# A gated adapter kernel in split fp32: W_up loaded by slot behind the first rows, its halves made by ACT and GpSimd, a new order for the first tiles and the tail

## The chip, the core and the metric

The kernel runs on one NeuronCore of a Trainium2 chip. Its engines are TensorE (PE, matrix products into PSUM), VectorE (DVE), ScalarE (ACT), GpSimd (POOL) and SyncE (SP, which here only issues DMAs). Each engine takes its instructions in the order in which they are written and waits on semaphores of the others. The metric is the device time of one execution in microseconds.

## What is computed

For each of 64 sequences (64 rows of 512 values) an expert index from 0 to 2 picks one set of adapter weights. All is fp32:

```python
Wd = W_down[stream]; bd = b_down[stream]; Wu = W_up[stream]
bu = b_up[stream]; g = ln_w[stream]; b = ln_b[stream]
residual = hidden_states
h = jnp.einsum('bsh,bhk->bsk', hidden_states, Wd) + bd[:, None, :]
h = jax.nn.gelu(h, approximate=False)
h = jnp.einsum('bsk,bkh->bsh', h, Wu) + bu[:, None, :]
h = residual + h
mean = jnp.mean(h, axis=-1, keepdims=True)
var = jnp.mean(jnp.square(h - mean), axis=-1, keepdims=True)
h = (h - mean) * jax.lax.rsqrt(var + LN_EPS)
return h * g[:, None, :] + b[:, None, :]
```

W_down is 512x256 and W_up 256x512 for each of the three experts.

## The kernel before, in words

**Tiles.** Two sequences of the same expert make a tile of 128 rows. The kernel sorts the sequences by expert on the chip (DVE and one small product, over at about 7 us), which gives 33 tiles in 66 slots. `io_table` holds the sequence of each slot, `tile_expert` the expert of each tile. Since tiles are sorted, W_up is kept by slots: slot 0 holds the expert of the first tile, `wu_from` says which experts the slots take.

**Precision.** Every factor is split into a high part (rounded to fp32r) and a low part (the rest), and a product is made of three: high x high, high x low, low x high. So W_down and W_up need a `wd_hi`/`wd_lo` and `wu_hi`/`wu_lo` of 128x1024 each per expert. Before the loop, all of this must be made from what the DMAs bring.

**One tile t** passes through these steps. PE `transpose_x(t)` (4 instructions) writes xT; ACT `x_hi` copies the high half and DVE `x_lo` makes the low one; PE `down(t)` makes 12 products into `h`; DVE `down_bias` adds the bias to `hb`; ACT `gelu` makes g; PE `transpose_g` (2); ACT `g_hi`, DVE `g_lo`; POOL `add_bias` makes xb = x + b_up; ACT `seed` copies xb into the PSUM bank of y; PE `up(t)` adds 6 products to it; DVE `stats`, `mean_var`, `variance`; POOL `power` makes rstd; DVE `scale` makes (y - mean) * ln_w into `scaled`; ACT `rescale` multiplies by rstd into `normed` (2 buffers); POOL `shift` adds ln_b into `res`; SP and ACT store one half each. The last two tiles take a shorter end on DVE, `shift_last`.

**Order.** Each engine's order is written by hand. PE does in body(t): transpose_g(t), down(t+1), transpose_x(t+3), up(t). ACT does in body(t): seed(t), g_hi(t-1), a store, gelu(t), x_hi(t+2), rescale(t-3), where rescale(k) waits for scaled(k), rstd(k) and, since normed has two buffers, for shift(k-2). POOL does in body(t): shift(t-1), power(t), add_bias(t+4). DVE does in body(t): stats(t-1), g_lo(t), down_bias(t+1), mean_var(t-1), variance(t-1), x_lo(t+2), scale(t-1). In front of these loops stand the first tiles by hand, between the copies of the weights.

**The weights in front.** ACT issues the loads of W_down and the first half of expert 0 of W_up; SP issues, behind the first x rows, the rest of W_up by expert (L244), then x rows, ln_w (L311), ln_b. ACT makes wd_hi of expert 0, POOL (L251) that of 1 and 2. ACT waits until all of W_up has landed, then makes the three wu_hi (L469); DVE makes all wd_lo (L256) and wu_lo (L686) and the down bias rows (L614). POOL's add_bias for tile 1 waits for the first wu_lo.

## Time and profile before

| | us |
|---|---|
| median of 3 executions | 142.57 |
| the three | 140.57, 142.57, 143.46 |
| the profiled execution | 140.62 |
| its span, first to last instruction | 138.5 |
| PE busy in it | 126.7 (91%) |
| DVE busy | 114.8 (83%) |
| POOL busy | 106.3 (77%) |
| ACT busy | 83.2 (60%) |

What lies around the span is 2.1 us. Two stages are to be told apart: up to about 30 us, weights and first rows arrive and PE works with gaps; from then on, PE runs one tile behind another without a gap up to 130 us; then a tail of 8 us. A busy share is a mean over all three, so the waits have to be read stage by stage. Of the DMA, 21.9 MB moved, at 293 to 350 GB/s from 3.5 to 24 us and at about half of that or less later.

### The profile page before, as it was taken

To read this page: it belongs to the slowest core of one execution; us is meant where nothing else is said; L and a number is where in the kernel's file an instruction comes from. 1 tells how busy PE (TensorE), PEld (TensorE's weight loads), DVE (VectorE), ACT (ScalarE), POOL (GpSimd) and SP (SyncE) were. 2 spreads that over 40 slices of the span, in tenths; PEclk is the share of its full clock that TensorE was granted. 3 is DMA by queue.
4 is the path that set the end of the run, shared out by engine and by line. 5 is a ranking of instruction groups with operands and counts; after the bars stand their busy time and mean duration, and the time that the engine had idled before them with its cause. 6 is when DMAs were issued, how large, how long until landed. Compare 5 with 4: busy or idle time off the path is not lost.

```text
span 138.5 us, 4090 instructions
## 1 busy us (share of the span) xinstructions
PE 126.7 (91%) x848; PEld 112.3 (81%) x849; DVE 114.8 (83%) x278; ACT 83.2 (60%) x174; POOL 106.3 (77%) x113
## 2 busy tenths in 40 slices
PE   6886888989999999999999999999999999999820
PEld 6785757859999999999999999999999999998610
DVE  1899595998888799888988897889788978897982
ACT  0834558457766666666666666766666666666600
POOL 7096049509888888888888889888888898889770
PEclk9999999999999999999999999999999999999995
DMA  1989999544233545555544555445546633332465
GB/s 39 331 293 325 350 300 301 159 122 146 80 116 114 156 145 157 146 158 145 151 160 126 163 161 163 153 151 151 151 151 151 151 76 76 80 76 51 98 167 143
DMA packets 13216, 21.94 MB, mean 158 GB/s; under 512 B 2313, under 2 KB 3858, under 8 KB 13202
## 3 DMA queue, kind: packets, MB, share of 16 engines
q1 hardware_dynamic: 8674, 15.48, 37.7%
q10 hardware_dynamic: 4528, 6.31, 16.4%
q8 instruction: 4, 0.07, 0.2%
q14 instruction: 10, 0.08, 0.2%
HBM read 13.39 MB, written 8.65 MB: 159 GB/s over the span
## 4 chain that ended last, share of the span: by engine, by line
PE 69%; DVE 7%; DMA 6%; ACT 4%; issue 3%; POOL 3%; DVEq 2%; SPq 2%; POOLq 1%; ACTq 0%
PE hg_ps L814 29%; PE y_ps L847 27%; PE xT_ps L800 9%; PE hg_ps L823 5%; DMA wu<-in_L_cond_W_up_dram 5%; POOL res L384 2%; DMA itok_all_i<-in_itok_B_dram 2%; DVE wu_lo L686 2%; ACT wu_hi L469 1%; DVE hb L637 1%; DVEq L607 1%; DVE r_stats L649 1%; SPq L241 1%; DVEq L61 1%; SPq L244 1%
## 5 line engine op out<-in xcount | busy, mean ns | idle before, releaser
L384 POOL TENSOR_TENSOR res<-normed,lnb_rows 128x512 f32<-128x512 f32 x31 | 40.0, 1290 | 15.3 <-ACT normed L465 15.1
L367 POOL TENSOR_TENSOR xb<-x_sb,bu_rows 128x512 f32<-128x512 f32 x33 | 44.7, 1356 | 6.6 <-DVE wu_lo L686 5.5
L445 ACT ACTIVATE g<-hb 128x256 f32<-128x256 f32 x33 | 13.8, 418 | 37.7 <-DVE hb L637 37.7
L649 DVE BATCH_NORM_STATS2 r_stats<-y_ps 128x6 f32<-128x512 f32 x33 | 23.0, 695 | 6.0 <-issue 5.1
L670 DVE SCALAR_TENSOR_TENSOR scaled<-y_ps,r_mv,lnw_rows 128x512 f32<-128x512 f32 x33 | 24.5, 743 | 0.1
L847 PE MATMUL y_ps<-wu_hi,gT_hi 128*128 x66 | 23.4, 435 | 0.7 <-ACT gT_hi L450 0.7
L814 PE MATMUL hg_ps<-wd_hi,xT_hi 128*128 x132 | 23.9, 303 | 0.0
L629 DVE TENSOR_TENSOR xT_lo<-xT_ps,xT_hi 128x512 fp32r<-128x512 f32 x33 | 22.8, 689 | 0.3 <-ACT xT_hi L440 0.2
L465 ACT ACTIVATE normed<-scaled,rstd 128x512 f32<-128x512 f32 x31 | 22.4, 724 | 0.0
L800 PE MATMUL xT_ps<-ident,x_sb 128*128 128x128 f32 x132 | 20.0, 274 | 1.8 <-DMA x_sb<-in_x_dram 1.8
L847 PE MATMUL y_ps<-wu_lo,gT_hi 128*128 x66 | 20.8, 397 | 0.4 <-DVE wu_lo L686 0.4
L814 PE MATMUL hg_ps<-wd_hi,xT_lo 128*128 x132 | 21.0, 281 | 0.0
L847 PE MATMUL y_ps<-wu_hi,gT_lo 128*128 x66 | 20.8, 396 | 0.2 <-DVE gT_lo L643 0.2
L814 PE MATMUL hg_ps<-wd_lo,xT_hi 128*128 x132 | 20.9, 281 | 0.0
L457 ACT COPY y_ps<-xb 128x512 f32<-128x512 f32 x33 | 19.5, 590 | 1.6 <-POOL xb L367 1.5
L440 ACT CAST xT_hi<-xT_ps 128x512 fp32r<-128x512 f32 x33 | 18.8, 571 | 2.0 <-PE xT_ps L800 2.0
L373 POOL TENSOR_TENSOR rstd<-var_eps,half_neg 128x1 f32<-128x1 f32 x33 | 18.1, 550 | 1.6 <-DVE var_eps L658 1.6
L637 DVE TENSOR_TENSOR hb<-hg_ps,bd_rows 128x256 f32<-128x256 f32 x33 | 14.0, 423 | 5.3 <-PE hg_ps L814 4.8
L814 PEld LDWEIGHTS hg_ps<-wd_hi,xT_hi 128*128 128x128 f32 x132 | 17.8, 189 | 0.1
L814 PEld LDWEIGHTS hg_ps<-wd_hi,xT_lo 128*128 128x128 f32 x132 | 17.9, 188 | 0.0
L814 PEld LDWEIGHTS hg_ps<-wd_lo,xT_hi 128*128 128x128 f32 x132 | 17.8, 188 | 0.0
L800 PEld LDWEIGHTS xT_ps<-ident,x_sb 128*128 128x128 f32 x132 | 15.0, 140 | 2.9 <-DMA x_sb<-in_x_dram 1.9
(85 smaller groups left out, 146.0 us busy)
## 6 DMA issues: line engine op xcount, KB each, us to landing
x_sb<-in_x_dram SPq DMA_DIRECT2D x64, 128.0 KB, 2.7
out_dram<-res ACTq DMA_DIRECT2D x33, 128.0 KB, 2.4
out_dram<-res SPq DMA_DIRECT2D x33, 128.0 KB, 2.3
wd<-in_L_cond_W_down_dram ACTq DMA_DIRECT2D x3, 512.0 KB, 4.8
wu<-in_L_cond_W_up_dram SPq DMA_DIRECT2D x2, 512.0 KB, 5.6
...
```

The lines of the kernel that those rows point to most:

```text
L367: pool.tensor_tensor(xb[:, c % DEEP, :], x_sb[:, c % FAR, :], bu_rows[:, ds(e * H, H)], ALU.add).then_inc(xb_ready, 1)
L373: pool.tensor_tensor(rstd[:, c % DEEP:c % DEEP + 1], var_eps[:, c % DEEP:c % DEEP + 1], half_neg[:], ALU.pow).then_inc(rstd_ready, 1)
L384: pool.tensor_tensor(res[:, c % FAR, :], normed[:, c % PAR, :], lnb_rows[:, ds(e * H, H)], ALU.add).then_inc(res_ready, 1)
L440: act.copy(xT_hi[:, c % PAR, :], xT_ps[c % PAR][:]).then_inc(xhi_ready, 1)
L457: act.copy(y_ps[c % YBANKS][:], xb[:, c % DEEP, :]).then_inc(seeded, 1)
L465: act.activation(normed[:, c % PAR, :], scaled[:, c % DEEP, :], ACT.Copy, scale=rstd[:, c % DEEP:c % DEEP + 1]).then_inc(normed_ready, 1)
L629: dve.tensor_tensor(xT_lo[:, c % PAR, :], xT_ps[c % PAR][:], xT_hi[:, c % PAR, :].bitcast(F32), ALU.subtract).then_inc(xlo_ready, 1)
L649: dve.bn_stats(r_stats[:, c % DEEP, :], y_ps[c % YBANKS][:]).then_inc(stats_ready, 1)
L670: dve.scalar_tensor_tensor(out=scaled[:, c % DEEP, :], in0=y_ps[c % YBANKS][:], scalar=r_mv[:, c % DEEP, 0:1], in1=lnw_rows[:, ds(e * H, H ...
L800: mm = pe.transpose(xT_ps[c % PAR][:, k * P:(k + 1) * P], x_sb[:, c % FAR, k * P:(k + 1) * P], ident[:])
L814: mm = pe.matmul(h, x_half[:, c % PAR, k * P:(k + 1) * P], w_half[:, ds(w0 + k * BN, BN)], start=(w_half is wd_hi and x_half is xT_hi and ...
L847: mm = pe.matmul(y_ps[c % YBANKS][:], g_half[:, c % PAR, k * P:(k + 1) * P], w_half[:, ds(w0 + k * H, H)], start=False, stop=(n == 2 and k ...
```

## The change

W_up is no longer loaded by expert ahead of all but the first rows. SP waits until the sort is done, reads `wu_from`, and loads slot by slot, with x rows in between and a semaphore for each slot: slot 0, x of tile 2, slot 1, x of tiles 3 and 4, slot 2, x of tile 5, ln_w, x of tile 6, ln_b. ACT makes all `wd_hi`, the down bias rows, two of the three up bias rows, and all `wu_hi` as each slot lands; DVE makes the third up bias row, all `wd_lo` and `wu_lo` of slot 0; POOL makes `wu_lo` of slots 1 and 2, behind add_bias(2) and add_bias(3). The first tiles have a new written order on PE, ACT and DVE; scale(0) (the first user of ln_w) and rescale(0) to rescale(2) stand later. In the sort one link of the chain goes. In the tail, the last two tiles are scaled in place in PSUM, `shift_last` of the second-last tile moves ahead of stats of the last, rescale moves ahead of the last gelu and power ahead of a shift.

The diff, cut to its core:

```diff
 SP
-            load_w_up(sp, 0, 1, KB)
-            for e in range(1, E):
-                load_w_up(sp, e, 0, KB)
+            sp.wait_ge(slots_ready, 2)
+            sp.reg_load(from_regs, wu_from[0:1, 0:E])
+            from_expert = [sp.snap(reg, min_val=0, max_val=E - 1 - slot) + slot for slot, reg in enumerate(from_regs)]
+            load_w_up(sp, 0, from_expert[0])
             load(2, 2, entries(2, 0, 2))
-            sp.dma_start(lnw_rows[:], rows_of(ln_w, P)).then_inc(lnw_in, 16)
+            load_w_up(sp, 1, from_expert[1])
             for t in range(3, 5):
                 load(t, t, entries(t, 0, 2))
+            load_w_up(sp, 2, from_expert[2])
+            load(5, 5, entries(5, 0, 2))
+            sp.dma_start(lnw_rows[:], rows_of(ln_w, P)).then_inc(lnw_in, 16)
+            load(6, 6, entries(6, 0, 2))
             sp.dma_start(lnb_rows[:], rows_of(ln_b, P)).then_inc(lnb_in, 16)
...
 POOL
-            for e in range(1, E):
-                w_down_high(pool, e).then_inc(wd_hi_rest, 1)
-            pool.wait_ge(bu_ready, E)
-            add_bias(0, 0)
-            pool.wait_ge(wu_lo_ready, 1)
-            for t in range(1, DEEP):
+            pool.wait_ge(bu_last_ready, 1)
+            pool.wait_ge(bu_ready, E - 1)
+            for t in range(3):
                 add_bias(t, t)
+            w_up_low(pool, 1).then_inc(wu_lo_rest, 1)
+            add_bias(3, 3)
+            w_up_low(pool, 2).then_inc(wu_lo_rest, 1)
...
 ACT
+            wd_high(1)
             for t in range(2):
                 load_half(act, t, 1, act.snap(head_regs[3 * t], min_val=0, max_val=B - 1))
-            for e in range(E):
-                keep_up_bias(e)
+            wd_high(2)
+            for part in range(len(bd_banks)):
+                keep_down_bias(part)
             x_hi(0, 0)
+            keep_up_bias(0)
             x_hi(1, 1)
-            seed(0, 0)
+            keep_up_bias(1)
+            wu_high(0)
             gelu(0, 0)
-            act.wait_ge(wu_in, 16 * (E + 1))
-            wu_high(0, sources[0])
+            seed(0, 0)
             g_hi(0, 0)
             x_hi(2, 2)
-            wu_high(1, sources[1])
+            wu_high(1)
+            gelu(1, 1)
+            g_hi(1, 1)
+            x_hi(3, 3)
+            seed(1, 1)
+            gelu(2, 2)
+            x_hi(4, 4)
+            seed(2, 2)
+            wu_high(2)
...
+            seed(4, 4)
+            rescale(0, 0)
+            g_hi(4, 4)
+            gelu(5, 5)
+            x_hi(7, 7)
+            seed(5, 5)
+            rescale(1, 1)
+            rescale(2, 2)
...
 DVE (front)
             x_lo(0, 0)
-            dve.wait_ge(bd_ready, len(bd_banks))
+            dve.wait_ge(up_spread, E)
+            dve.tensor_copy(bu_rows[:, (E - 1) * H:E * H], y_ps[E - 1][:]).then_inc(bu_last_ready, 1)
             x_lo(1, 1)
+            dve.wait_ge(bd_ready, len(bd_banks))
             down_bias(0, 0)
...
-            wu_low(0, sources[0])
+            w_up_low(dve, 0).then_inc(wu_lo_first, 1)
             g_lo(0, 0)
             down_bias(1, 1)
             x_lo(2, 2)
-            wu_low(1, sources[1])
...
 DVE (tail)
             stats(last - 1, last - 1)
-            g_lo(last, last)
             dve.wait_ge(stats_ready, last)
             mean_var(last - 1, last - 1)
             variance(last - 1, last - 1)
-            scale(last - 1, last - 1, e_last[1])
+            g_lo(last, last)
+            scale_last(last - 1, e_last[1])
+            shift_last(last - 1, e_last[1])
             stats(last, last)
             dve.wait_ge(stats_ready, last + 1)
             mean_var(last, last)
             variance(last, last)
-            scale(last, last, e_last[0])
-            shift_last(last - 1, e_last[1])
+            scale_last(last, e_last[0])
             shift_last(last, e_last[0])
...
 PE
-            body(1, 1)
+            e_up, e_down = experts_from(1)
+            down(2, 2, e_down)
+            transpose_g(1, 1)
+            transpose_x(4, 4)
+            up(1, 1, e_up)
             body(2, 2)
```

**Order on ACT, tiles 3 to 6.** ACT before, from g_hi(2) to g_hi(4). In the names, gT_hi is g_hi, g is gelu, xT_hi is x_hi, y_ps is seed (its number is the tile modulo 4) and normed is rescale:

```order
L450 CAST gT_hi<-hg_ps0 128x256 [waits gT_ready]
L445 ACTIVATE g<-hb 128x256 [waits hb_ready]
L440 CAST xT_hi<-xT_ps1 128x512 [waits xT_ready]
L465 ACTIVATE normed<-scaled,rstd 128x512 [waits rstd_ready,scaled_ready]
L457 COPY y_ps0<-xb 128x512 [waits scaled_ready,xb_ready]
L450 CAST gT_hi<-hg_ps1 128x256 [waits gT_ready]
L445 ACTIVATE g<-hb 128x256 [waits hb_ready]
L440 CAST xT_hi<-xT_ps0 128x512 [waits xT_ready]
L465 ACTIVATE normed<-scaled,rstd 128x512 [waits rstd_ready,scaled_ready]
L457 COPY y_ps1<-xb 128x512 [waits scaled_ready,xb_ready]
L450 CAST gT_hi<-hg_ps0 128x256 [waits gT_ready]
```

and in the changed kernel, from gelu(4) to g_hi(5):

```order
L444 ACTIVATE g<-hb 128x256 [waits hb_ready]
L439 CAST xT_hi<-xT_ps0 128x512 [waits xT_ready]
L456 COPY y_ps0<-xb 128x512 [waits scaled_ready,xb_ready]
L464 ACTIVATE normed<-scaled,rstd 128x512 [waits rstd_ready,scaled_ready]
L449 CAST gT_hi<-hg_ps0 128x256 [waits gT_ready]
L444 ACTIVATE g<-hb 128x256 [waits hb_ready]
L439 CAST xT_hi<-xT_ps1 128x512 [waits xT_ready]
L456 COPY y_ps1<-xb 128x512 [waits scaled_ready,xb_ready]
L464 ACTIVATE normed<-scaled,rstd 128x512 [waits rstd_ready,scaled_ready]
L464 ACTIVATE normed<-scaled,rstd 128x512 [waits res_ready,rstd_ready,scaled_ready]
L456 COPY y_ps2<-xb 128x512 [waits scaled_ready,xb_ready,slots_ready]
L449 CAST gT_hi<-hg_ps1 128x256 [waits gT_ready]
```

Before, one rescale stands in each tile (rescale(0) behind gelu(3), rescale(1) behind gelu(4)); now rescale(0) stands behind seed(4), and rescale(1) and rescale(2) stand together behind seed(5), both ahead of seed(6) and g_hi(5).

**Order on POOL, tiles 0 to 2 of its loop.** POOL in the changed kernel (it is the same as before here, but for line numbers; res is shift, rstd is power, xb is add_bias):

```order
L381 TENSOR_TENSOR res<-normed,lnb_rows 128x512
L370 TENSOR_TENSOR rstd<-var_eps,half_neg 128x1 [waits var_ready]
L208 TENSOR_LOAD tile_expert
L364 ISA [waits seeded,x_in5]
L364 TENSOR_TENSOR xb<-x_sb,bu_rows 128x512
L208 TENSOR_LOAD tile_expert
L381 ISA [waits normed_ready]
L381 TENSOR_TENSOR res<-normed,lnb_rows 128x512
L370 TENSOR_TENSOR rstd<-var_eps,half_neg 128x1 [waits var_ready]
L208 TENSOR_LOAD tile_expert
L364 ISA [waits seeded,x_in6]
L364 TENSOR_TENSOR xb<-x_sb,bu_rows 128x512
```

Behind shift(0) stand power(1) and add_bias(5), behind shift(1) power(2) and, next, add_bias(6).

**Order on POOL in front.** Before, from the copies of W_down to add_bias(1):

```order
L251 CAST wd_hi<-wd 128x1024 [waits wd_in1]
L251 CAST wd_hi<-wd 128x1024 [waits wd_in2]
L207 TENSOR_LOAD tile_expert [waits bu_ready,slots_ready]
L367 ISA [waits x_in0]
L367 TENSOR_TENSOR xb<-x_sb,bu_rows 128x512
L207 TENSOR_LOAD tile_expert [waits wu_lo_ready]
L367 ISA [waits x_in1]
L367 TENSOR_TENSOR xb<-x_sb,bu_rows 128x512
```

and now, from add_bias(2) to power(0):

```order
L208 TENSOR_LOAD tile_expert
L364 ISA [waits x_in2]
L364 TENSOR_TENSOR xb<-x_sb,bu_rows 128x512
L258 TENSOR_TENSOR wu_lo<-wu,wu_hi 128x1024 [waits wu_hi_ready]
L208 TENSOR_LOAD tile_expert
L364 ISA [waits x_in3]
L364 TENSOR_TENSOR xb<-x_sb,bu_rows 128x512
L258 TENSOR_TENSOR wu_lo<-wu,wu_hi 128x1024 [waits wu_hi_ready]
L370 TENSOR_TENSOR rstd<-var_eps,half_neg 128x1 [waits var_ready]
```

The two casts of W_down and the wait for DVE's first wu_lo are gone from POOL, and two subtractions of 128x1024 stand ahead of power(0).

## Rows read from the trace of the kernel before

**Rows 1.** Windows: us, busy and instructions of PE, PEld, DVE, ACT, POOL, clock, DMA.
```profile
40.00:130.00 90.00, 90.00 (x621) 81.61 (x619) 78.05 (x183) 59.93 (x130) 79.33 (x79) 1.00 0.47 131
...
134.00:135.00 1.00, 0.00 (x0) 0.00 (x0) 1.00 (x2) 0.00 (x0) 0.33 (x1) 0.83 0.67 205
```

**Rows 2.** Chain that ended last, around tile 4 (start us, us, what).
```profile
29.85 0.44 PE hg_ps L823 x2
...
33.64 0.22 PE hg_ps L823 x2
33.86 1.42 PE hg_ps L814 x12
35.27 0.44 PE xT_ps L800 x4
35.71 1.40 PE y_ps L847 x6
```

**Rows 3.** Timeline of ACT, tiles 3 to 6 (start us, us, instruction).
```profile
29.21 0.42 ACT L445 ACTIVATE g<-hb 128x256 f32<-128x256 f32 x1 [2.83 <-DVE hb L637]
...
30.00 0.72 ACT L465 ACTIVATE normed<-scaled,rstd 128x512 f32<-128x512 f32 x1
...
32.47 0.42 ACT L445 ACTIVATE g<-hb 128x256 f32<-128x256 f32 x1 [0.95 <-DVE hb L637]
...
34.06 0.59 ACT L457 COPY y_ps<-xb 128x512 f32<-128x512 f32 x1
...
37.36 0.59 ACT L457 COPY y_ps<-xb 128x512 f32<-128x512 f32 x1
...
37.87 0.37 ACT L450 CAST gT_hi<-hg_ps 128x256 fp32r<-128x256 f32 x1
```

**Rows 4.** Timeline of POOL, tiles 0 to 5.
```profile
30.96 1.29 POOL L384 TENSOR_TENSOR res<-normed,lnb_rows 128x512 f32<-128x512 f32 x1 [4.13 <-ACT normed L465]
32.20 0.55 POOL L373 TENSOR_TENSOR rstd<-var_eps,half_neg 128x1 f32<-128x1 f32 x1
32.73 1.30 POOL L367 TENSOR_TENSOR xb<-x_sb,bu_rows 128x512 f32<-128x512 f32 x1
34.16 1.29 POOL L384 TENSOR_TENSOR res<-normed,lnb_rows 128x512 f32<-128x512 f32 x1
```

**Rows 5.** Timeline of TensorE, tiles 0, 1 and 5.
```profile
12.22 0.66 PE L800 MATMUL xT_ps<-ident,x_sb 128*128 128x128 f32 x4 [0.20 <-DMA x_sb<-in_x_dram]
...
13.08 0.72 PE L814 MATMUL hg_ps<-wd_hi,xT_hi 128*128 x4
...
16.23 0.38 PE L823 MATMUL hg_ps<-ident,g 128*128 128x128 f32 x2
...
38.93 0.71 PE L847 MATMUL y_ps<-wu_hi,gT_hi 128*128 x2
```

**Rows 6.** POOL instructions of line L367: duration ns min/median/max.
```profile
L367 POOL TENSOR_TENSOR xb<-x_sb,bu_rows x33: 1278/1297/2274, 11.5 to 126.2; 128x512 f32<-128x512 f32 x33
```

**Rows 7.** Groups by line: xcount, busy us, mean ns, idle before.
```profile
L469 ACT CAST wu_hi<-wu 128x1024 fp32r (+1 forms) x3 | 3.1, 1049 | 0.5 <-DMA wu<-in_L_cond_W_up_dram 0.5
```

**Rows 8.** SP queue, start us and us of its issues.
```profile
7.29 1.29 SPq L241 DMA_DIRECT2D x_sb<-in_x_dram  x2
8.64 1.69 SPq L244 DMA_DIRECT2D wu<-in_L_cond_W_up_dram  x3
11.06 1.14 SPq L241 DMA_DIRECT2D x_sb<-in_x_dram  x2
```

**Rows 9.** DMA issues: KB each, median us from issue to landing.
```profile
x_sb<-in_x_dram SPq DMA_DIRECT2D x64, 128.0 KB, 2.7
...
wu<-in_L_cond_W_up_dram SPq DMA_DIRECT2D x2, 512.0 KB, 5.6
...
x_sb<-in_x_dram ACTq DMA_DIRECT2D x2, 128.0 KB, 3.5
```

**Rows 10.** Timeline of DVE, its last two instructions.
```profile
134.41 1.41 DVE L679 SCALAR_TENSOR_TENSOR res<-scaled,rstd,lnb_rows 128x512 f32<-128x512 f32 x2
```

More of the change, by code:

```diff
@@ L155, in adapter_program @@
         wd_in = [sem(f"wd_in{e}") for e in range(E)]
-        wu_in = sem("wu_in")
+        wu_in = [sem(f"wu_in{slot}") for slot in range(E)]
         biases_in = sem("biases_in")
@@ L301, in _ @@
             head_regs = [sp.alloc_register(f"head{i}") for i in range(4)]
+            from_regs = [sp.alloc_register(f"from{i}") for i in range(E)]
             sp.wait_ge(slots_ready, 1)
```

155 lines of the change are left out of this document (87 added, 68 removed).

## Prediction

> **What bounds the kernel now.** I read the busy times by stretch first: from 40 to 130 us PE is busy 90.00 of 90.00 us at full clock [rows 1]. The chain that ended last confirms it: transpose_g 0.22, down 1.42, transpose_x 0.44 (the step from there to 35.71), up 1.40, together 3.48 us per tile, with nothing between [rows 2]. No edit touches those instructions, so the kernel's time is when this run begins, plus what breaks it, plus the tail.
>
> It begins at transpose_g(3), 29.85 [rows 2]. PE's first product is at 13.08 [rows 5]. Up to 29.85 it has four downs, three ups, three transposes of g and four of x to do: 5.7 + 4.2 + 0.7 + 1.8 = 12.4 us in 16.8. So 4.4 us of waits can be won there at most, beside an earlier first product.
>
> Then I looked for what runs beside PE with little slack, since a hand-written order can break there. The timelines of ACT and POOL show a ring: rescale(0) at 30.00 [rows 3], shift(0) at 30.96, power(1) 32.20, add_bias(5) 32.73 to 34.03, shift(1) 34.16 [rows 4], seed(5) at 34.06, 0.03 behind add_bias(5), and seed(6) at 37.36, then g_hi(5) at 37.87 [rows 3], and up(5) at 38.93 [rows 5]. g_hi(5) is over at 38.24, so the ring stands 0.7 us ahead of PE. It is hidden, but nearly as long as PE's tile.
>
> **The change, front.** What it removes: POOL's two casts of W_down and its wait for DVE's wu_lo, two wu_lo and the down bias copies on DVE, and ACT's wait for all of W_up. What it adds to ACT: two more casts of 1.05 us [rows 7] and the bias copies. I walk it by tile.
>
> x of tile 1 has less ahead of it in the DMA queues (no part of W_up). The two x loads of ACT took 3.5 us to land, the median of all x loads is 2.7 [rows 9]: 0.8 us earlier, so transpose_x(1) is at 11.4 in place of 12.22, down(0) behind it by the same 0.86 at 12.3, and down(1) is over at 15.4 (3.15 us from 13.08 to 16.23 [rows 5]). The bounds are no gain (12.22) and, if a load takes 2.3, 11.0. ACT's third cast and the bias copies end before 11.4, behind W_down's last landing; that cover is about 0.3 us.
>
> Slot 0 of W_up: SP's x issues end at 8.58; a register load on SP takes about 0.7 (10.33 to 11.06), so it is issued at 9.3 [rows 8]. 512 KB take 5.6 under load [rows 9] and more likely somewhat less here, since the queues are emptier: landed at 14.0 (bounds 13.3 and 14.9). ACT: wu_high(0) 14.05 to 15.0, gelu(0) at once behind, 15.4. POOL's add_bias(0) waits for the last bias row from DVE (about 13.5) and a register load, 14.0 to 15.3; DVE's wu_lo(0) has two operands in SBUF and waits for it. I take that from add_bias itself, whose longest is 2.27 against a median of 1.30 [rows 6]: one of the two engines stood still there. wu_lo(0) is then done at 16.5. Seed(0) and g_hi(0) end at 16.4, up(0) runs 16.45 to 17.85.
>
> Then transpose_x(3) to 18.3, down(2) to 19.7, transpose_g(1) to 20.1. ACT does g_hi(1), x_hi(3), seed(1) in this order, about 0.4 + 0.5 + 0.6 (0.51 from a 512-column start to the next [rows 3]): PE waits 1.2 us, up(1) 21.6 to 23.0. ACT goes on with gelu(2), x_hi(4), seed(2) and wu_high(2), 22.8 to 23.9. Slot 2 has landed by then: SP issues it at about 16.0. POOL's subtraction for slot 2 starts at 23.9. The trace shows no 128x1024 subtraction on POOL; twice a 128x512 of 1.28 to 1.30 [rows 6] is 2.55 (bounds 2.1 and 3.0). It ends at 26.45, up(2)'s second pair of products waits for it, and transpose_g(3) follows 0.95 later: **27.4 in place of 29.85, a lead of 2.45 us**. With the bounds above the lead is 1.3 to 3.0.
>
> The Trainium skill (GPSIMD Engine Reference, "Elementwise — side-by-side cycle accounting") gives 4497 ns for such an add of 2048 columns; an estimate from it for 1024 is 2.25 us, and the lead by it would be 2.75. No row here shows that size.
>
> Behind this I cost at nothing: ln_w later (issued about 18.4; scale(0) stands at about 26.2, so the cover is near 1 us if it takes 7 us to land), ln_b (shift(0) is at 32), the shorter sort (one link of 0.2 us, some 0.1 of it won, behind the DMAs), DVE's later scale(0) to scale(2) (0.74 each, PE waits for none of them directly).
>
> **The change, the ring.** Here the new order costs. rescale(0) now stands behind gelu(4), x_hi(6) and seed(4), not behind gelu(3). Before, gelu(4) started 2.62 us after transpose_g(3) (32.47 against 29.85), and PE still paces it. From a gelu to the rescale behind it were 0.79 (29.21 to 30.00 [rows 3]); with a seed between, 0.79 + 0.51 = 1.30. So rescale(0) is at transpose_g(3) + 3.92. From there the old trace gives each step: to shift(0) 0.96, to power(1) 1.24, to add_bias(5) 0.53, its own 1.30 and 0.03 to seed(5), 4.06 in all [rows 3, 4]; seed(5) to rescale(1) 0.51; the same 4.06 again over shift(1), power(2), add_bias(6) to seed(6); 0.51 to g_hi(5), 0.37 for it and 0.1 to PE. Sum: 3.92 + 4.06 + 0.51 + 4.06 + 0.51 + 0.47 = 13.53. rescale(2) lies between, waits for power(2) and is over before add_bias(6) is. Before, up(5) started 38.93 - 29.85 = 9.08 behind transpose_g(3). **PE, which has nothing else to do ahead of up(5), stands still for 4.45 us once.** up(5) starts at 27.4 + 13.53 = 40.93, 2.0 us later than before. The lead is eaten and 2.0 more; with the bounds of the lead +1.45 to +3.15. Behind up(5) all goes on at 3.48.
>
> **The change, the clock.** Such a gap has a second price. PE's last product releases DVE at 132.6 [rows 10], and the granted clock of 134 to 135 us is 0.83 [rows 1]: full to 134.66, then the 1.2 GHz level, 2.1 us behind the last product. A gap of 4.45 us is twice that, so I expect the clock to have fallen when up(5) comes. How soon it comes back no row shows. The only stretch at half rate is the last 3.84 us; as long a stretch would cost 1.9 us, and nothing is the other bound. I take 1.5, nearer the upper one. The Trainium skill (TensorE: Matmul & The Clock Gate, "HAM oscillation") says that waits between bursts drop TensorE to half rate, and that it pays for this when work returns; the fall at 134.66 agrees.
>
> **The tail.** shift_last(31), one of two of 0.7 us [rows 10], moves ahead of stats(32); but it needs about 0.6 of the time between stats(31) and y(32), which g_lo(32) and scale_last(31) already fill, so stats(32) comes 0.6 later and the chain behind it is 0.7 shorter. Won: 0.1 (bounds 0 and 0.4).
>
> **Sum.** -2.45 + 4.45 + 1.5 - 0.1 = +3.4 us on the profiled execution's 140.62: **144.0**. That execution is at the low end of the three; the median is 1.95 higher, and the same sum against it gives 145.9. Nothing in the trace tells me which of the two a new median resembles, so I name the middle, **145.0**. As a ratio it is 2.4% slower.
>
> **Rivals.** (A) The gap comes but the clock holds: 144.0 - 1.5 = 142.5 on the profiled basis, 1.4% slower, within 2%. For it: the clock was full through all the smaller waits of the front. Against it: the fall at 134.66. 0.2. (B) On the other side, faster: the ring stays hidden and the lead is kept. 140.62 - 2.45 - 0.1 = 138.1, faster by 1.8%; with the lead's upper bound 137.5, 2.2%. It needs rescale(0) 4.45 us earlier against PE, before gelu(4); or power(2) would have to come without shift(1). It decides where transpose_g(3) is at or before 25.4: from there the stall is paid by the lead. Every bound of the walk together gives 26.8. 0.1. (C) The front doesn't win: if slot 0 lands at 14.9 and POOL's two subtractions take 3.0 each, transpose_g(3) is at 28.6, and the same ring gives 145.2 on the profiled basis, 3.2% slower. For it: W_up is issued later than before. 0.1. My forecast, gap and clock both: 0.6.
>
> **Chances.** Changes below about 2% can't be told from none here. The forecast's own range on the profiled basis is 141.5 to 145.7 (+1.45 to +3.15, clock 0 to 1.9, tail); its middle is at 2.4%, so of its 0.6 I put 0.42 beyond 2% and 0.18 within. A gives 0.2 within (0.01 beyond, rounded off), B 0.03 faster and 0.07 within, C 0.1 slower. Faster 0.03, raised to 0.05 for what I did not see; within 0.43; slower 0.52. The range of the time: 141.5 below, and 145.7 with the median's offset, 147.5, above.
>
> **What would show it.** Right: transpose_g(3) near 27.4; one gap of PE of 4 to 5 us ahead of up(5), with ACT waiting for POOL in rescale(2) and seed(6); granted clock under 1.00 in the slices behind it; PE without a gap after that. Wrong: up(5) within 3.5 us of up(4), or transpose_g(3) later than 28.6, or a wait of DVE for ln_w. If add_bias and shift overlap or rescale(0) comes before gelu(4) is through, the sum falls with the 4.45.

## The result and the profile after

The kernel after takes 145.5 us (median of 4 executions, 144.43 to 146.48), the kernel before beside it 141.72 (4 executions, 140.57 to 143.46): a ratio of 1.032, 95% interval 1.027 to 1.037. It is **slower by 3.2%**. The profiled execution of after took 146.48, its span is 144.3 us, 5.8 more than before's 138.5.

The page's slices of the kernel after (40 equal ones of 3.6 us, tenths of busy time; PEclk is the granted clock):

```profile
PE   6899896899619999999999999999999999999840
PEclk9999999999975899999999999999999999999999
```

One hole in PE, in slices 11 and 12; the clock is low from the end of the hole on, in slices 12 to 14. The windows (columns as in [rows 1]):

```profile
40.00:50.00 10.00, 7.35 (x30) 6.44 (x31) 4.77 (x13) 4.95 (x11) 7.61 (x8) 0.66 0.30 91
50.00:130.00 80.00, 80.00 (x555) 72.72 (x554) 69.17 (x162) 53.60 (x116) 70.11 (x69) 1.00 0.48 136
```

From 50 us on PE is again busy all the time, as before from 40 [rows 1]. The timeline rows around the hole, ACT first, then POOL, then PE (start us, us, what, idle before and who ended it); [rows 3 to 5] are their counterparts:

```profile
33.09 0.72 ACT L464 ACTIVATE normed<-scaled,rstd 128x512 f32<-128x512 f32 x1
37.13 0.59 ACT L456 COPY y_ps<-xb 128x512 f32<-128x512 f32 x1 [0.82 <-POOL xb L364]
37.66 0.72 ACT L464 ACTIVATE normed<-scaled,rstd 128x512 f32<-128x512 f32 x1
40.74 0.72 ACT L464 ACTIVATE normed<-scaled,rstd 128x512 f32<-128x512 f32 x1 [2.36 <-issue]
41.62 0.59 ACT L456 COPY y_ps<-xb 128x512 f32<-128x512 f32 x1 [0.17 <-POOL xb L364]
```

```profile
34.05 1.28 POOL L381 TENSOR_TENSOR res<-normed,lnb_rows 128x512 f32<-128x512 f32 x1 [4.28 <-ACT normed L464]
...
38.55 1.26 POOL L381 TENSOR_TENSOR res<-normed,lnb_rows 128x512 f32<-128x512 f32 x1 [1.45 <-ACT normed L464]
40.28 1.26 POOL L364 TENSOR_TENSOR xb<-x_sb,bu_rows 128x512 f32<-128x512 f32 x1
```

```profile
29.25 0.43 PE L870 MATMUL hg_ps<-ident,g 128*128 128x128 f32 x2
37.95 0.60 PE L847 MATMUL xT_ps<-ident,x_sb 128*128 128x128 f32 x4
42.65 1.22 PE L894 MATMUL y_ps<-wu_hi,gT_hi 128*128 x2 [4.10 <-ACT gT_hi L449]
48.26 0.60 PE L847 MATMUL xT_ps<-ident,x_sb 128*128 128x128 f32 x4
```

The ring of the prediction stands here link by link: rescale(0) 33.09, shift(0) 34.05, add_bias(5) 35.81, seed(5) 37.13, rescale(1) 37.66, shift(1) 38.55, add_bias(6) 40.28, seed(6) 41.62, g_hi(5) 42.15, up(5) 42.65. Between transpose_x(8), over at 38.55, and up(5) PE has nothing, 4.10 us. The chain that ended last runs through the same place:

```profile
39.77 0.55 POOL rstd L370
40.32 1.24 POOL xb L364
...
42.65 2.92 PE y_ps L894 x6
...
46.00 2.42 PE hg_ps L861 x12
```

Six products of an up take 2.92 us there and twelve of a down 2.42, where [rows 2] has 1.40 and 1.42: half rate for the up, and a little better for the down, since the full clock came back before its end. By microsecond (same columns as the windows above):

```profile
41.00:42.00 1.00, 0.00 (x0) 0.00 (x0) 0.00 (x0) 0.83 (x2) 0.91 (x2) 0.64 0.03 8
47.00:48.00 1.00, 1.00 (x7) 1.00 (x6) 0.00 (x0) 0.00 (x0) 1.00 (x1) 0.50 0.54 176
48.00:49.00 1.00, 1.00 (x9) 0.96 (x9) 0.43 (x2) 0.00 (x0) 0.07 (x1) 0.95 0.22 70
```

0.50 is the 1.2 GHz level. The clock fell at about 41.3, while PE stood still, and was back at 48.1 (both worked out from the shares 0.64 and 0.95).

**The 5.8 us add up.** transpose_g(3) is 0.60 earlier (29.25; 29.85 [rows 2]). up(5) starts 13.40 behind it in place of 9.08: + 4.32. From up(5) to transpose_x(9) it takes 5.61 (42.65 to 48.26); before, 3.12 (38.93 [rows 5] to the next row below): + 2.49. From there to the end of DVE's last res nothing changes. What is left, 0.4, lies behind DVE's last instruction, which ends 2.27 us ahead of the span's end now and 2.68 before ([rows 10]: 134.41 + 1.41). -0.60 + 4.32 + 2.49 - 0.41 = 5.80. Two rows of the kernel before that belong to this, transpose_x(9) and the stats of the last tile, which PE's last product released (0.27 us of waiting, so at 132.6; the prediction used it and pointed at [rows 10], where it doesn't stand):

```profile
42.05 0.60 PE L800 MATMUL xT_ps<-ident,x_sb 128*128 128x128 f32 x4
132.60 0.70 DVE L649 BATCH_NORM_STATS2 r_stats<-y_ps 128x6 f32<-128x512 f32 x1 [0.27 <-PE y_ps L847]
```

### The profile page after: what moved, and what is told of

Its sections match the earlier page's. It is cut to its first block, busy times and chain, and to the rows that moved or that the text cites. A ratio compares the mean times of both kernels' runs of the same rounds, so it can differ in the third digit from the quotient of the medians.

```text
span 144.3 us, 4085 instructions
## 1 busy us (share of the span) xinstructions
PE 130.2 (90%) x850; PEld 116.8 (81%) x851; DVE 111.7 (77%) x275; ACT 85.7 (59%) x177; POOL 106.4 (74%) x113
## 4 chain that ended last, share of the span: by engine, by line
PE 62%; POOL 4%; DVE 3%; issue 1%; ACT 1%; POOLq 1%; ACTq 1%; DVEq 0%
PE hg_ps L861 25%; PE y_ps L894 25%; PE xT_ps L847 7%; PE hg_ps L870 4%; POOL res L381 2%; DVE res L718 1%; POOL rstd L370 1%; POOL xb L364 1%; DVE y_ps L709 1%; POOLq L208 1%; ACT normed L464 0%; DVE r_stats L682 0%; ACTq L433 0%; DVE hb L670 0%; ACT y_ps L456 0%
## 5 line engine op out<-in xcount | busy, mean ns | idle before, releaser
L364 POOL TENSOR_TENSOR xb<-x_sb,bu_rows 128x512 f32<-128x512 f32 x33 | 43.7, 1326 | 12.6 <-ACT bu_rows L486 12.6
L894 PE MATMUL y_ps<-wu_hi,gT_hi 128*128 x66 | 23.9, 444 | 6.3 <-ACT gT_hi L449 5.1
L703 DVE SCALAR_TENSOR_TENSOR scaled<-y_ps,r_mv,lnw_rows 128x512 f32<-128x512 f32 x31 | 22.9, 743 | 0.0
L861 PE MATMUL hg_ps<-wd_lo,xT_hi 128*128 x132 | 21.4, 285 | 0.0
L676 DVE TENSOR_TENSOR gT_lo<-hg_ps,gT_hi 128x256 fp32r<-128x256 f32 x33 | 13.8, 418 | 7.8 <-ACT gT_hi L449 7.5
L861 PEld LDWEIGHTS hg_ps<-wd_hi,xT_hi 128*128 128x128 f32 x132 | 18.3, 194 | 0.3 <-issue 0.2
L861 PEld LDWEIGHTS hg_ps<-wd_lo,xT_hi 128*128 128x128 f32 x132 | 18.3, 192 | 0.0
```

What stands on the lines that cost most here:

```text
L364: pool.tensor_tensor(xb[:, c % DEEP, :], x_sb[:, c % FAR, :], bu_rows[:, ds(e * H, H)], ALU.add).then_inc(xb_ready, 1)
L703: dve.scalar_tensor_tensor(out=scaled[:, c % DEEP, :], in0=y_ps[c % YBANKS][:], scalar=r_mv[:, c % DEEP, 0:1], in1=lnw_rows[:, ds(e * H, H ...
L861: mm = pe.matmul(h, x_half[:, c % PAR, k * P:(k + 1) * P], w_half[:, ds(w0 + k * BN, BN)], start=(w_half is wd_hi and x_half is xT_hi and ...
L894: mm = pe.matmul(y_ps[c % YBANKS][:], g_half[:, c % PAR, k * P:(k + 1) * P], w_half[:, ds(w0 + k * H, H)], start=False, stop=(n == 2 and k ...
```

## Experiments on the ring and the clock

### The ring undone in the kernel after

```diff
             x_hi(5, 5)
             seed(3, 3)
+            rescale(0, 0)
...
             seed(4, 4)
-            rescale(0, 0)
+            rescale(1, 1)
...
             seed(5, 5)
-            rescale(1, 1)
             rescale(2, 2)
```

> The kernel after, with ACT's rescales of tiles 0, 1 and 2 each one tile earlier (rescale(0) behind seed(3), rescale(1) behind seed(4), rescale(2) behind seed(5)), as they stood in the kernel before; the rest of the change is kept. Theory (ring): rescale(0) comes at transpose_g(3) - 0.4 and not at + 3.84, so shift, power and add_bias run beside PE again. No gap ahead of up(5): it starts at 38.3 (29.25 + 9.08) in place of 42.65, granted clock 1.00 in every slice from 2 to 130 us, span 144.3 - 4.3 - 2.6 = 137.4, about 0.8% under the kernel before (its span is 138.5). Rival (the gap has another cause, the later ln_w and ln_b loads or DVE's later scales): the gap of about 4 us stays, span over 142.

Measured: 139.3 us (138.82 to 140.22), ratio to before 0.984 (0.980 to 0.988), span 138.2, clock without a low slice:

```profile
PEclk9999999999999999999999999999999999999998
```

Two instructions on ACT, rescale(0) and rescale(1), one tile earlier each, take 6 us off the kernel after; rescale(2) stands behind seed(5) in both, though the expectation counts it among the moved. The hole and the low clock are gone, so the cause holds; the rest of the change is worth 1.6% against before. The profiled execution is the longest of the six: its span missed the expected 137.4 by 0.8, while the spans of the six run from 136.8 to 138.2, with a median of 137.3. What held the profiled one up, POOL's timeline says:

```profile
31.52 1.30 POOL L381 TENSOR_TENSOR res<-normed,lnb_rows 128x512 f32<-128x512 f32 x1 [2.15 <-DMA lnb_rows<-in_L_cond_ln_b_dram]
38.72 0.73 PE L894 MATMUL y_ps<-wu_hi,gT_hi 128*128 x2 [0.39 <-ACT gT_hi L449]
```

The second row is PE's up(5). shift(0) waits for ln_b now, which the change had moved behind x of tile 6. I had costed that at nothing because shift(0) was "at 32"; it was hidden only by the ring's own delay.

### The ring alone, in the kernel before

Several statements are put on one line here:

```diff
-            for t in range(2, STORE_B_LAG):
-                body(t, t)
+            body(2, 2)
+            seed(3, 3); g_hi(2, 2); gelu(3, 3); x_hi(5, 5)
+            g_hi(3, 3); gelu(4, 4); x_hi(6, 6); seed(4, 4); rescale(0, 0)
+            g_hi(4, 4); gelu(5, 5); x_hi(7, 7); seed(5, 5); rescale(1, 1); rescale(2, 2)
```

> The kernel before with the new order of ACT for tiles 3 to 5 alone: seed, g_hi, gelu and x_hi as in the kernel after, rescale(0) behind seed(4), rescale(1) and rescale(2) behind seed(5). Theory (ring): transpose_g(3) stays at 29.85, up(5) starts 13.4 behind it at 43.25 in place of 38.93, PE has one gap of 4.1 to 4.4, the clock falls and costs 2.6: span 138.5 + 4.3 + 2.6 = 145.4, 4.9% slower. Rival (the new order hurts only together with the later ln_w and ln_b or DVE's later scales): gap under 2 us, clock full, span under 141.

Measured: 148.32 us (147.05 to 149.43), ratio 1.044 (1.036 to 1.051), span 146.1. PE's timeline, transpose_g(3), up(5), transpose_x(9):

```profile
30.39 0.43 PE L837 MATMUL hg_ps<-ident,g 128*128 128x128 f32 x2 [0.20 <-ACT g L445]
43.90 1.21 PE L861 MATMUL y_ps<-wu_hi,gT_hi 128*128 x2 [4.18 <-ACT gT_hi L450]
49.61 0.64 PE L814 MATMUL xT_ps<-ident,x_sb 128*128 128x128 f32 x4
```

13.51 from transpose_g(3) to up(5), and 5.71 in place of 3.12 behind it. The new order of ACT in tiles 3 to 5 costs 4.4% without anything else of the change, with ln_w and ln_b as early as they ever were. It moves rescale(0) and rescale(1) one tile later, and seed(4) and seed(5) from ahead of g_hi to behind x_hi. The experiment before, which put back the two rescales and left the seeds where the change has them, shows that the rescales make the gap.

### Only rescale(2) moved

```diff
             rescale(1, 1)
-            rescale(2, 2)
...
                     g_hi(t - 1, c - 1)
+                if isinstance(t, int) and t == STORE_B_LAG:
+                    rescale(2, 2)
```

> The kernel after, with rescale(2) alone moved behind g_hi(5), so that ACT stands no longer in it while POOL works on power(2). Theory (ring): add_bias(6), which POOL reaches only behind shift(1) and power(2), is what up(5) waits for by way of seed(6); so up(5) starts at 42.65 within 0.1, or 0.1 to 0.2 earlier for the time rescale(2) itself kept ACT from seed(6), gap 4.0 to 4.1, span 144.3 within 0.5. Rival (two rescales in a row block ACT, 2.36 us idle ahead of rescale(2), and that makes the gap): g_hi(5) comes 2 to 3 us earlier, gap 1 to 2 us.

Measured (one execution): 145.1 us, span 143.1. ACT now stands 3.58 us ahead of seed(6), which waits for xb, and not in rescale(2), and PE is no better off (up(5)):

```profile
42.17 1.22 PE L895 MATMUL y_ps<-wu_hi,gT_hi 128*128 x2 [4.44 <-ACT gT_hi L449]
```

up(5) is 13.74 behind transpose_g(3) (28.43), so the gap is no smaller: the long wait at rescale(2) in the timeline of after (2.36 us, the longest on ACT there) is a wait beside the path. The span is 1.2 shorter than after's: the front was 0.8 earlier in this execution and the clock cost 1.46 (4.58 for 3.12), not 2.49, which together is 1.85; the ring was 0.34 longer, and the end behind DVE's last res 0.29. That it stood outside the 0.5 expected is the front and the clock, not rescale(2).

### The gap filled with products, twice

The first try:

```diff
+                if c == 5 and isinstance(t, int) and t == 5:
+                    pe.wait_ge(xlo_ready, 8)
+                    warm_up(34, xT_ps[1])
                 up(t, c, e_up)
```

> The kernel after, with 34 products of 128x128 on constants added on PE between transpose_x(8) and up(5), into a free bank that nobody reads: the gap is there as before, but PE is not idle in it. (PE's first six tiles are written out ahead of the loop, for which nothing else changes.) Theory (the clock has its own price, beside the gap's): up(5) starts at 42.65 within 0.2, the granted clock stays 1.00 from 40 to 50 us, the 5.61 us from up(5) to transpose_g(7) become 3.0, span 144.3 - 2.6 = 141.7. Rival (half rate has another cause than PE's idleness): granted clock under 1.00 behind the gap all the same, span 144 to 145.

Measured: 154.66 us, span 151.4. It missed on two mistakes of mine: x_lo(7), for which the filler waits, stands behind g_lo(5) on DVE and so behind the gap; and one such product is two records of 0.11, not one, so 34 of them are 7.6 us at full clock. The clock fell here too (0.50 from 43 to 45 us), so they took 9.0, from 42.82 to up(5) at 51.86. They filled nothing (the window that this row is from ends before they do, at 51 of their 68 records):

```profile
42.82 7.38 PE L806 MATMUL xT_ps<-ones 128*128 128x128 f32 x51 [5.71 <-DVE xT_lo L662]
```

The second try waits for something that is there early, and has half the products:

```diff
+                if isinstance(t, int) and t == 5:
+                    pe.wait_ge(scaled_ready, 4)
+                    for _ in range(17):
+                        mm = pe.matmul(y_ps[3][:, 0:P], ones[:], ones[:], start=False, stop=True,
+                                       skip_group_check=True)
+                    mm.then_inc(filled, 1)
                 up(t, c, e_up)
```

> The kernel after, with 17 products of 128x128 on constants added on PE between transpose_x(8) and up(5), into the bank of y(3), which is free from scale(3) to seed(7) (the first filler stood behind x_lo(7), which comes only after the gap; this one waits for scale(3), over at 36.9). At 0.225 us each (0.90 for the four of the front) they fill 3.8 us of the gap of 4.1. Theory (the clock's fall comes of PE's idleness and has a price of its own): up(5) stays at 42.65 within 0.3, granted clock 1.00 from 40 to 50 us, up(5) to transpose_x(9) take 3.1 in place of 5.61, span 141.0 to 142.0. Rival (the fall has another cause): clock under 1.00 behind the gap all the same, span over 143.

Measured: 143.02 us (142.44 to 143.1), ratio 1.008 (1.001 to 1.015), span 141.2. PE's filler, up(5), transpose_x(9), and a window behind:

```profile
37.65 3.96 PE L926 MATMUL y_ps<-ones 128*128 128x128 f32 x34
41.94 0.73 PE L897 MATMUL y_ps<-wu_hi,gT_hi 128*128 x2 [0.33 <-ACT gT_hi L450]
45.09 0.60 PE L850 MATMUL xT_ps<-ident,x_sb 128*128 128x128 f32 x4
42.00:43.00 1.00, 1.00 (x5) 0.83 (x6) 0.97 (x5) 0.38 (x2) 1.00 (x3) 1.00 0.61 186
```

up(5) is still 13.30 behind transpose_g(3), which was at 28.64 here, 0.6 earlier than in after; the ring is untouched. But up(5) to transpose_x(9) takes 3.15. The clock column has 1.00 from 37 to 50 us. Work that nobody uses made the kernel 2.5 us faster than after's 145.5 (a ratio of 1.008 to the kernel before beside it, where after had 1.032). So the clock's price is its own, beside the gap's, and in this place PE's idleness is its cause.

## Experiments on the front and the tail

### The kernel after once more

No edit.

> The kernel after once more, unchanged, for a second profile. Theory: the 0.60 us of lead at transpose_g(3) in its first profile was one execution's: PE spread the biases there at 0.21 us a product (the kernels with the same code up to there: 0.12), so transpose_x(0) began at 12.19 and not at 10.7. Now transpose_g(3) at 28.4 to 28.9 (lead 1.0 to 1.4, as in the experiments with the same front), up(5) 13.3 to 13.8 behind it, clock at half for 3.4 or 6.8 us behind the gap, span 142.5 to 144.5. Rival (the front's lead is 0.6 by the kernel itself): transpose_g(3) at 29.2 again.

Measured: 145.81 us (145.51 to 146.04), ratio 1.038 (1.032 to 1.045), span 143.7. transpose_g(3) came at 29.15, as the rival said, and not at 28.4 to 28.9; the span is in the expected range. PE's timeline: transpose_x(0), up(0), transpose_x(3), down(2), up(1), the second products of up(2), transpose_g(3), up(5), transpose_x(9); then a window:

```profile
10.72 0.63 PE L847 MATMUL xT_ps<-ident,x_sb 128*128 128x128 f32 x4
16.65 0.73 PE L894 MATMUL y_ps<-wu_hi,gT_hi 128*128 x2 [0.20 <-ACT gT_hi L449]
18.98 0.66 PE L847 MATMUL xT_ps<-ident,x_sb 128*128 128x128 f32 x4 [0.67 <-DMA x_sb<-in_x_dram]
...
19.79 0.76 PE L861 MATMUL hg_ps<-wd_hi,xT_hi 128*128 x4
23.39 0.72 PE L894 MATMUL y_ps<-wu_hi,gT_hi 128*128 x2 [1.21 <-ACT y_ps L456]
28.07 0.70 PE L894 MATMUL y_ps<-wu_lo,gT_hi 128*128 x2 [0.48 <-POOL wu_lo L258]
29.15 0.43 PE L870 MATMUL hg_ps<-ident,g 128*128 128x128 f32 x2
42.57 1.03 PE L894 MATMUL y_ps<-wu_hi,gT_hi 128*128 x2 [4.12 <-ACT gT_hi L449]
47.27 0.60 PE L847 MATMUL xT_ps<-ident,x_sb 128*128 128x128 f32 x4
42.00:43.00 1.00, 0.43 (x2) 0.36 (x3) 0.54 (x2) 0.43 (x2) 1.00 (x2) 0.90 0.04 8
```

The lead at transpose_g(3) is 0.70, though transpose_x(0) began 1.5 us earlier than in the first profile of after (12.19 there). An early start alone doesn't give the lead. But "by the kernel itself" is too much, since four other experiments have the same code up to transpose_g(3). Side by side (us):

| profile | up(0) at | PE's wait for x of tile 3 | up(0) to transpose_g(1) | from there to transpose_g(3) | transpose_g(3) at |
|---|---|---|---|---|---|
| forecast | 16.45 | none | 3.25 | 7.7 | 27.4 |
| after | 18.07 | none | 3.36 | 7.82 | 29.25 |
| after once more | 16.65 | 0.67 | 4.71 | 7.79 | 29.15 |
| ring undone | 16.58 | 0.39 | 4.43 | 7.80 | 28.81 |
| gap filled, second try | 16.64 | 0.25 | 4.28 | 7.72 | 28.64 |
| rescale(2) moved | 17.22 | none | 3.40 | 7.81 | 28.43 |
| gap filled, first try | 16.80 | none | 3.43 | 7.72 | 27.95 |

So the same front leads by 0.6 to 1.9 us, and what varies are two things: when PE gets to up(0), and whether it then waits for x of tile 3. Where it does neither much, in the first try at the filled gap, transpose_g(3) comes at

```profile
27.95 0.38 PE L870 MATMUL hg_ps<-ident,g 128*128 128x128 f32 x2
```

In the second profile of after, the clock was low from 42.8 to 46.2 (the slice of 46 to 47 has 0.89): it fell 0.2 us after up(5) had begun. up(5) to transpose_x(9) took 4.70, a price of 1.58.

### Seeds ahead of g_hi(1)

The front experiments from here to the bias copies stand on the kernel with the ring undone. Its profiled span of 138.2, from which they forecast, is that of its longest execution; the median of the six is 137.3.

```diff
             gelu(1, 1)
+            seed(1, 1)
+            seed(2, 2)
             g_hi(1, 1)
             x_hi(3, 3)
-            seed(1, 1)
             gelu(2, 2)
             x_hi(4, 4)
-            seed(2, 2)
             wu_high(2)
```

> The first experiment's kernel (rescales undone, span 138.2) with ACT's seed(1) and seed(2) moved ahead of g_hi(1), into ACT's idle time of 2.53 us there. PE's wait of 1.20 ahead of up(1) goes (up(1) 21.9 in place of 23.03) and transpose_g(3) comes at 27.7 in place of 28.81. Theory (ln_b's landing holds the ring: shift(0) at 31.52 waited for that transfer, not for ACT): shift(0) stays at 31.5, so up(5) stays within 0.3 of 38.72 and the span within 0.3 of 138.2. Rival (the front's lead carries through): span 137.1.

Measured: 139.23 us (139.11 to 139.63), ratio 0.983 (0.976 to 0.989), span 137.1. That is the rival's number, but not by its mechanism, and it is no gain over the median span of 137.3. The 1.20 us ahead of up(1) went, but came back at up(2), since POOL's low half of slot 2 hangs on ACT's cast behind x_hi(4) (PE, then POOL):

```profile
27.29 0.70 PE L894 MATMUL y_ps<-wu_lo,gT_hi 128*128 x2 [1.03 <-POOL wu_lo L258]
24.77 2.39 POOL L258 TENSOR_TENSOR wu_lo<-wu,wu_hi 128x1024 fp32r<-128x1024 f32 x1 [1.99 <-ACT wu_hi L469]
```

transpose_g(3) came at 28.37, 0.44 earlier instead of 1.1. ln_b landed 0.9 earlier in this execution (shift(0) at 30.58) and let the ring follow. The median is the same within the intervals.

### ln_w and ln_b ahead of x of tile 5

```diff
             load_w_up(sp, 2, from_expert[2])
-            load(5, 5, entries(5, 0, 2))
             sp.dma_start(lnw_rows[:], rows_of(ln_w, P)).then_inc(lnw_in, 16)
-            load(6, 6, entries(6, 0, 2))
             sp.dma_start(lnb_rows[:], rows_of(ln_b, P)).then_inc(lnb_in, 16)
-            for t in range(7, STORE_A_LAG):
+            for t in range(5, STORE_A_LAG):
```

> The first experiment's kernel (rescales undone, span 138.2) with the issues of ln_w and ln_b moved ahead of those of x of tiles 5 and 6, right behind slot 2 of W_up: ln_b is issued at 18.1 in place of 21.25, 3.1 earlier. Theory (ln_b's landing holds the ring): shift(0) at 29.3 to 29.8 in place of 31.52, the small waits of PE ahead of up(3) to up(5) go, transpose_g(6) at 28.81 + 3 x 3.48 = 39.25 in place of 40.23, span 137.2. Rival (x of tile 5 now comes late, or ln_b lands no earlier, since the queue is full): span 138.2 or more.

Measured: 141.26 us (139.81 to 142.43), ratio 0.987 (0.977 to 0.998), no better than the 0.984 it stands on; the expected 1 us didn't come. The rival may be right: in the profiled execution PE waited 3.16 us for x of tile 5. But that was one of two long executions (142.4; the other two took 139.8 and 140.1), so it doesn't explain the rest, and the cause stays open.

### wu_high(2) earlier, and ln_b one place earlier

```diff
             x_hi(3, 3)
+            wu_high(2)
             gelu(2, 2)
             x_hi(4, 4)
-            wu_high(2)
```

> The kernel with the early seeds (span 137.1) and, in addition, ACT's wu_high(2) ahead of gelu(2) and x_hi(4), right behind x_hi(3): slot 2 of W_up has landed by 21.8 there, and POOL idled 1.99 us for that cast ahead of its wu_lo(2), for which PE then stood 1.03 us in up(2). Theory (front): POOL's wu_lo(2) at 23.5 in place of 24.77, PE's 1.03 us gone, transpose_g(3) at 27.3 in place of 28.37. Theory (ln_b holds the ring): shift(0) still waits for ln_b's landing, 30.6 to 31.5, and up(5) starts 7.2 behind that as there, so the span stays at 137.1 to 138.0 although the front is 1 us shorter. Rival (shift(0) and ring have slack, the front's lead carries through): span 136.0.

Measured: 139.3 us (138.36 to 140.7), ratio 0.983 (0.977 to 0.989). Its profile, the shortest execution, has a span of 136.3, near the rival's 136.0; the median doesn't follow: transpose_g(3) at 26.65, all of PE's wait for POOL gone, but then

```profile
29.96 1.29 POOL L381 TENSOR_TENSOR res<-normed,lnb_rows 128x512 f32<-128x512 f32 x1 [2.75 <-DMA lnb_rows<-in_L_cond_ln_b_dram]
37.13 0.73 PE L894 MATMUL y_ps<-wu_hi,gT_hi 128*128 x2 [0.38 <-ACT gT_hi L449]
```

up(5) is 7.17 behind shift(0), as in the kernel with the ring undone (7.20). Of the 1.7 us by which the front is shorter than with the early seeds alone (28.37), 0.7 reach transpose_g(6) (38.64 against 39.30), and nothing reaches the median. With ln_b ahead of x of tile 6:

```diff
-            load(6, 6, entries(6, 0, 2))
             sp.dma_start(lnb_rows[:], rows_of(ln_b, P)).then_inc(lnb_in, 16)
-            for t in range(7, STORE_A_LAG):
+            for t in range(6, STORE_A_LAG):
```

> The same with ln_b's issue one place earlier, ahead of x of tile 6 (and not, as in the experiment that lost 3.2 us, ln_w and ln_b ahead of x of tile 5). Theory (ln_b holds the ring): ln_b issued 1.3 to 2.4 earlier, lands at about 29.4, shift(0) with it, up(5) about 36.6, span 136.0 to 136.5, 3% under the kernel before; x of tile 6 lands by 28.5 and is needed at 29.0. Rival (the queues are full, so that the order only moves the wait): PE waits for x of tile 6 ahead of transpose_x(6), span 137 or more.

Measured: **138.2 us** (137.2 to 138.65), before beside it 141.91, ratio 0.972 (0.966 to 0.977): the fastest kernel of this study, 2.8% under before. Its profiled execution has transpose_x(0) only at 12.75 (a late start, as in the first profile of after, below), and still a span of 136.6. shift(0) waits 0.99 us for ln_b there, and not 2.75.

So ln_b's landing was the next limit, as it seemed: a front shorter by 1.7 us did nothing for the median alone, one place in SP's queue then gave 1.1.

### The bias copies earlier

```diff
+            keep_up_bias(0)
+            keep_up_bias(1)
             x_hi(0, 0)
-            keep_up_bias(0)
             x_hi(1, 1)
-            keep_up_bias(1)
```

and the same for DVE's copy and x_lo(0).

> The fastest kernel so far (seeds, wu_high(2) and ln_b earlier) with the copies of the up biases out of PSUM ahead of the first x work: ACT's two ahead of x_hi(0), where ACT idled 0.4 to 1.8 us for PE, and DVE's one ahead of x_lo(0). Theory (add_bias(0) is released by these copies, and seed(0) and up(0) by it; the prediction's walk had left out ACT's second one): POOL's add_bias(0) 0.5 to 1.4 us earlier against transpose_x(0), PE's wait of 0.2 to 0.5 ahead of up(0) goes, span 0.2 to 0.5 less. Rival (the copies now stand ahead of x_hi(0), x_lo(0) and so of down(0)): down(0) 0.3 later, no gain or a loss of up to 0.3.

Measured: 139.03 us, ratio 0.987 (0.974 to 1.000), executions from 137.71 to 143.62. For the time that is inconclusive: five of the seven executions took 137.7 to 139.6, no better than the 138.2 it stands on. The profile is of the longest one, and it shows two things. The copies do what the theory says: add_bias(0) starts 2.95 us behind transpose_x(0) (14.07 and 11.12), in place of 3.54 to 3.57 in the fastest kernel and in the second profile of after, and PE's wait ahead of up(0) is gone. up(0) itself comes no earlier against transpose_x(0) (6.07; 5.89 and 5.93 there), since PE waited 0.43 for x of tile 1. And the execution is long because x of tile 6, which this kernel loads behind ln_b, came late:

```profile
32.51 1.12 PE L846 MATMUL xT_ps<-ident,x_sb 128*128 128x128 f32 x4 [3.12 <-DMA x_sb<-in_x_dram]
```

with the clock at half behind it, from 31.3 to 38.1 us.

### The tail alone, in the kernel before

The change's edits of the tail, applied to before: the last two scales in place in PSUM, shift_last(31) ahead of stats(32), power(29) ahead of shift(28), rescale(29) ahead of gelu(32).

```diff
             stats(last - 1, last - 1)
-            g_lo(last, last)
             dve.wait_ge(stats_ready, last)
...
+            g_lo(last, last)
-            scale(last - 1, last - 1, e_last[1])
+            scale_last(last - 1, e_last[1])
+            shift_last(last - 1, e_last[1])
             stats(last, last)
```

> The kernel before with the change's tail alone: the last two tiles' scale kept in the banks of y, shift_last(31) ahead of stats(32), POOL's power(29) ahead of shift(28), ACT's rescale(29) ahead of gelu(32). Theory (as predicted): what shift_last gives behind stats(32) it takes ahead of it; from transpose_g(32) to the end of DVE's last res, 5.96 us before, 5.9 to 6.0 now; time within 0.3% of the kernel before. Rival (the tail gains what the sum of the kernel after lacks): 0.4 to 0.6 us, 0.3 to 0.4% faster, with DVE's last res ending 5.4 to 5.6 behind transpose_g(32).

Measured: 140.94 us (140.23 to 142.49), ratio 0.994 (0.987 to 1.001), span 138.2. PE's transpose_g(32), DVE's stats(32) and its last res:

```profile
129.87 0.38 PE L829 MATMUL hg_ps<-ident,g 128*128 128x128 f32 x2
133.15 0.69 DVE L649 BATCH_NORM_STATS2 r_stats<-y_ps 128x6 f32<-128x512 f32 x1
135.09 0.75 DVE L685 SCALAR_TENSOR_TENSOR res<-y_ps,rstd,lnb_rows 128x512 f32<-128x512 f32 x1
```

stats(32) is 0.55 later than before's 132.60 and the last res ends at 135.84, where before has 135.82. DVE gains nothing, as the theory says; the interval of the time holds both the theory's nothing and the rival's 0.3 to 0.4%, so it doesn't decide. The last store gains a little: from DVE's end to the end of the span it takes 2.36 here, 2.2 to 2.6 in the eleven other profiles with the new tail, and 2.68 and 2.78 in the two with the old one, where the stores of both last tiles leave together.

## Why the prediction was right, and where it was not

**The sign and its cause were right.** One gap ahead of up(5), ACT waiting for POOL in rescale(2) and seed(6), low clock behind it and nothing after: all as forecast. 145.0 was named, 145.5 measured; 2.4% slower was named, 3.2% measured.

**The ring: right to 0.2 us.** 13.53 was summed from rows; measured were 13.40 and 13.42 (after), 13.51 (alone, in before), 13.30 (gap filled) and 13.74 (rescale(2) moved). It could be summed so well because all its terms were already in the timelines of before; what had to be seen was that it had 0.7 us of slack, and what the new place of rescale(0) does to that. That it was closed from both sides, undone in after and added alone to before, is the strongest evidence of this study. Rival B (the ring stays hidden) is out: the gap came in every kernel with the new order. Its sign, transpose_g(3) at or before 25.4, only says when the lead would pay for the gap; the best front of this study had it at 26.65.

**The front: the term was mis-sized.** 2.45 us of lead, with bounds 1.3 to 3.0, against 0.60 and 0.70 in the two profiles of after, and 0.6 to 1.9 in the six profiles with this front. transpose_g(3) at 29.25 and 29.15 is also later than 28.6, which the prediction had named as a sign of being wrong, and later than rival C had it. Rival C (the front doesn't win) names 145.2 us and comes near, but not by its conditions: POOL's subtraction took 2.39 and not 3.0, and ACT cast slot 0 at 13.30 in the second profile, so that it had landed well before 14.9. The walk was right up to up(0) in the second profile (16.45 forecast, 16.65 there; 18.07 in the first, where PE started late), and it was right on PE's wait of 1.2 (1.21) and on the way from transpose_g(1) to transpose_g(3) (7.7; 7.8). It fails between up(0) and transpose_g(1). In the second profile this went as follows. transpose_g(1) came at 21.36 and not at 19.7: PE waited 0.67 for x of tile 3, which the change puts behind slot 1 of W_up in SP's queue, a step moved whose price I never wrote down; up(0), transpose_x(3) and down(2) took 1.66, 0.81 and 1.57, and not the 1.40, 0.45 and 1.4 of a PE that runs without a stop (together 0.8 more; each is the time from its start to the next one's, less the wait); and up(0) itself was 0.2 late. That is 1.66 of the 1.75 us missing; 0.1 is lost behind transpose_g(1). In the first profile there was no such wait, and up(0) to transpose_g(1) took 3.36 for 3.25; there the late start was the loss. POOL's subtraction took 2.39, for 2.55 assumed. The Trainium skill (GPSIMD Engine Reference, "Elementwise — side-by-side cycle accounting") gives the 4497 ns from which the prediction's estimate of 2.25 came; the trace lies between the two. The change also issues one idle product more to PE ahead of transpose_x(0) (four, which take 0.9 us, and not three), which neither the description of the change nor the walk has. The walk also left out that ACT's second bias copy releases add_bias(0), which started at 14.29 for 14.0. The lock I took from add_bias's durations is there: DVE's low half of slot 0 takes 1.8 to 2.2 us beside POOL's add_bias, 1.2 for wd_lo of the same size without.

**The clock: the mechanism right, the size too small.** I took 1.5, and 1.9 as the upper bound, from the 3.84 us at half rate at the end of before. The price was 2.49 and 1.58 in the two profiles of after, 2.59 and 1.46 with the ring alone and with rescale(2) moved. The bound was no bound: that stretch ended with the program, not with the clock's return. Nor was the fall 2.1 us behind the last product a measure: in the tail of after it came 5.0 us behind it (PE's last product is over at 138.67; the clock falls at about 143.7):

```profile
143.00:144.00 1.00, 0.00 (x0) 0.00 (x0) 0.00 (x0) 0.00 (x0) 0.00 (x0) 0.84 0.13 45
```

That the clock fell in all five profiles with the unfilled gap bears the forecast out, but on a thinner basis than the prediction thought. The Trainium skill (TensorE: Matmul & The Clock Gate, "HAM oscillation") says that waits between bursts cost half rate once work returns; the traces agree, 5.61 behind the gap in after and 3.15 where it was filled. Rival A (the clock holds) is out.

**Costed at nothing, wrongly: ln_b.** In after it is hidden by the ring itself, so the number didn't suffer. With the ring undone it is what PE waits for next, by way of shift(0).

**The tail:** 0.1 forecast. Behind DVE's last res the twelve profiles with the new tail took 2.2 to 2.6, before 2.68, so 0.05 to 0.45 was won, all of it in the last store and none in the DVE rows that I summed.

**How the sum came near all the same.** On the profiled execution's basis it said 144.0 and the profile of after took 146.48: 2.5 too low (lead 1.85, clock 1.0, ring and tail -0.4). The median came out at 145.5, as the profiled execution of before is at the low end of its kernel, as I had said, and that of after at the high end. The middle between two bases covered a part of the error, and that part is luck. It is a near number with two wrong terms in it, and both erred to the same side. The working has small slips too, none of which changes the direction: the bounds as stated give 141.7 to 145.7 and a middle 2.1% above, not 2.4%; rival C's 4.6 us are 3.3%; and 145.0 is 1.7% above the 142.57 then known, where the 2.4% is 3.4 on 140.62.

What stays open: why executions of the kernel before spread from 140.2 to 145.0 us, and how often the kernels with ln_b ahead of an x row (137.2 to 143.6 over three of them) pay for it by a late x. Two profiled executions do, by 3.16 us for x of tile 5 and 3.12 for x of tile 6; one, of the fastest kernel, doesn't. The kernel before ranged as widely beside the last of them, so the late x is no full account of the spread.
